# Attention row maxima from the high halves alone, two heads at a time in two 32-row groups of TensorE, with two score banks instead of three

## The chip, the cores and the metric

One core of one Trainium2 chip runs the whole kernel. The metric is the device time of one execution, in microseconds (us); lower is better.

## The reference, cut to what matters

The input x (2 x 1024 x 1024) is normalised over its last axis. Grouped-query attention follows: 32 query heads and 8 key/value heads of 32 numbers, rotary embedding, causal mask, softmax. A gated feed-forward net with 4-bit weights is computed from the same normalised x, and the two are joined:

```python
scores = einsum('bqhd,bkhd->bhqk', q, k) / sqrt(32) + causal_mask
attn = softmax(scores, axis=-1)
s = einsum('bhqk,bkhd->bqhd', attn, v) @ wo
x = x + s * silu(ffn(layernorm(x)))
```

The change touches only how the maximum of each row of scores is found, which the softmax subtracts before the exponential, and what stands around that.

## The kernel before

The stages run one after the other: project_qkv, attend, project_out, feed_forward. All products use numbers split into a 16-bit high half and a 16-bit low half. Only `attend` is changed, and `load_heads`, which fills its buffers.

**Tiling.** There are 64 heads in all (2 batches of 32). A step works on one head of 1024 positions, cut into ST = 8 tiles of 128, which are visited in ORDER = 7, 0, 6, 1, 5, 2, 4, 3. Four heads share one key head; `qT[:, u]` and `kT[:, u]` (u = 0 or 1) hold such a group of four. Their partitions are a stack of three pieces of 32 rows: q high with k high, q high with k low, q low with k high, so one matmul with 96 rows gives the full product.

**What a head costs.** `maxima` on TensorE computes, for query tile t, the scores of its 128 queries against keys 0 to (t+1)·128 into a PSUM tile (a wide one of 1024 columns and a narrow one of 512, in turn), adds the causal mask by a 128-column matmul (L670), and VectorE's `tensor_reduce` (L793) takes the negated maximum of each row: 8 such rounds in a head. When 8 are there, `turn_shifts` transposes the 8 columns (L654), ScalarE copies them out (L754), and SyncE sends them by DMA (L602) into row 96 of `qT`, against a row of ones in `kT`. So the score matmul with 97 rows (`scores`, L685) yields shifted scores, transposed (keys on partitions). There are 12 such chunks in a head, in 3 PSUM banks in turn, 8 of them with a mask matmul (L688). ScalarE takes the exponential of each chunk (L744) into `probs`. `probs` is split: its upper bits are the high half, and the low half `p_lo` is computed by GpSimd (POOL) in four parts of 1152, 1152, 1152 and 640 columns and by VectorE in one of 512 (all L580). `outputs` on TensorE (L712 to L716) multiplies both halves with the values, 80 matmuls of 32 to 65 columns in a head. ScalarE copies the result out (`copy_sums`, L764 and L766).

**Order.** Each engine runs its own program, in order. Step r of TensorE interleaves, over i = 0 to 7, `scores` of head r, `maxima` of head r+2, and `outputs` of head r-1; the transpose for head r+1 stands at i = 1. VectorE does the reductions of head r+2 and, after the first of them, its part of `p_lo` of head r-1. Waits are counting semaphores written by hand: maxima number n waits until number n-2 is reduced, a score chunk until the exponential three chunks back is done. The loop body holds 8 heads. The first 8 and the last 8 heads are written out, and the loop runs 6 times between them, so its body is jumped back to 5 times.

**Refill.** After the last score chunk of the fourth head of a group SyncE refills that half of `qT` and `kT` by 6 DMAs (`load_heads`, L91 and L92). The first `maxima` of the new group stand two to three steps later.

Of the kernel before, what the change touches and what calls it, by code (L numbers as in the profile page):

```python
# [7 lines left out]
ALU = mybir.AluOpType  # L8
# [506 lines left out]
def attend(nc, q_d, k_d, v_d, o_d, wo, ident, identb, maskb, qT, kT, qk_loaded, vn, v_loaded, o, o_stored, a, a_loaded,  # L515
# [7 lines left out]
    SC_BANKS = 3  # L523
# [5 lines left out]
    with ExitStack() as ctx:  # L529
# [3 lines left out]
        def sem(name):  # L533
# [6 lines left out]
        shift = sb("shift", [P, 2, ST], F16)  # L540
        shT = sb("shT", [P, 2, P], F16)
        sc_ps = [ctx.enter_context(nc.psum_tensor(f"sc_ps{i}", [P, BANK], F32)) for i in range(SC_BANKS)]
        mx_ps = [ctx.enter_context(nc.psum_tensor("mx_wide_ps", [P, FULL], F32)),
                 ctx.enter_context(nc.psum_tensor("mx_ps", [P, BANK], F32))]
# [6 lines left out]
        mx_taken = sem("mx_taken")  # L551
        shift_turned = sem("shift_turned")
# [16 lines left out]

        def chunks_to(t):  # L570

            return max(i + 1 for i, c in enumerate(SC) if c[0] == t)
# [10 lines left out]
        def steps(eng, step):  # L583

            for r in range(-3, 0):
                step(*at(0, 0, r, R))
# [9 lines left out]
        def _(sp):  # L596
            def send_shift(m, r):
                if not exists(m, r):
                    return
                h, u, q = head(m, r), r // REP, r % REP  # L600
                sp.wait_ge(shift_copied, h + 1)
                sp.dma_start(qT[STACK:STACK + 1, u, q, :], shT[STACK:STACK + ST, r % 2, :]  # L602
                             ).then_inc(shift_loaded[r % 2], 16)
# [26 lines left out]
            def step(m, r):  # L630
                send_shift(*at(m, r, 1, R))
# [14 lines left out]
        def _(pe):  # L646
            def turn_shifts(m, r):
                if not exists(m, r):
                    return
                h = head(m, r)  # L650
                pe.wait_ge(mx_taken, ST * (h + 1))
                if not isinstance(m, int) or h >= 1:
                    pe.wait_ge(shift_copied, h)
                pe.transpose(tr_ps[STACK:STACK + ST, 0:P], shift[:, r % 2, :], ident[:, :]).then_inc(shift_turned, 1)  # L654

            def maxima(m, r, i):
                if not exists(m, r):
                    return
                h, u, q, t = head(m, r), r // REP, r % REP, ORDER[i]
                if i == 0 and q == 0:  # L660
                    pe.wait_ge(qk_loaded[u], 96 * (m + 1))
                if not isinstance(m, int) or ST * h + i >= 2:
                    pe.wait_ge(mx_taken, ST * h + i - 1)
                n = (t + 1) * P
                bank = mx_ps[i % 2]
                for c in range(0, n, BANK):
                    e = min(c + BANK, n)
                    last = pe.matmul(bank[:, c:e], qT[0:STACK, u, q, t * P:(t + 1) * P], kT[0:STACK, u, c:e],  # L668
                                     start=True, stop=(e < n))
                last = pe.matmul(bank[:, t * P:n], identb[:, :], maskb[:, :], start=False, stop=True)  # L670
                last.then_inc(mx_ready, 1)

            def scores(m, r, i):
# [3 lines left out]
                if i == 0:  # L677
                    pe.wait_ge(shift_loaded[r % 2], 16 * ((R // 2) * m + r // 2 + 1))
# [55 lines left out]
        def _(act):  # L734
# [12 lines left out]
            def shifts(m, r):  # L747
                if not exists(m, r):
                    return
                h = head(m, r)  # L750
                act.wait_ge(shift_turned, h + 1)
                if not isinstance(m, int) or h >= 2:
                    act.wait_ge(shift_loaded[r % 2], 16 * ((R // 2) * m + r // 2))
# [1076 lines left out]
```

## Time and profile before

| what | value |
|---|---|
| median of 3 runs | 2586.61 us (2580.41 to 2593.28) |
| the profiled execution's own time | 2587.13 us |
| its span in the profile | 2584.2 us |
| PE (TensorE matmul) busy | 2391.5 us, 93% |
| DVE (VectorE) busy | 1550.2 us, 60% |
| POOL (GpSimd) busy | 942.3 us, 36% |
| ACT (ScalarE) busy | 748.2 us, 29% |

Times in profile rows count from the start of the span. The attention stage lies between about 389 and 932 us. A PE matmul record overlaps the next one, so that the pitch between two starts, and not the duration, tells what a matmul costs. The number in square brackets behind a row is the idle time of the engine just before it, with what ended it; "issue" means that the profile shows nothing that it waited for.

### The profile page before, as it was taken

The page shows a single profiled execution, that of the slowest core. Times are in us where ns is not written, and L with a number is a line of the kernel's source. Part 1 is how long each engine was busy: PE and PEld are TensorE (multiplying, and loading weights), DVE is VectorE, ACT ScalarE, POOL GpSimd, SP SyncE. Part 2 cuts the span into 40 slices and gives each one's busy share as a digit, 9 for nine tenths or more (in the row PEclk, how much of TensorE's full clock was granted, in tenths as well). Part 3 has the DMA queues.
Part 4 walks back from the last instruction along what each step waited for, and adds up shares of the span by engine and source line. Part 5 has one row for each costly group of instructions (what it writes and reads, how often), then busy time and mean ns, then how long its engine had stood idle before and what let it go on. Part 6 is the DMA issues. An engine that isn't in the chain of part 4 may idle for free.

```text
span 2584.2 us, 46178 instructions
## 1 busy us (share of the span) xinstructions
PE 2391.5 (93%) x17048; PEld 1234.9 (48%) x17048; DVE 1550.2 (60%) x2800; ACT 748.2 (29%) x1469; POOL 942.3 (36%) x619
## 2 busy tenths in 40 slices
PE   5877888999999959989999999999999999999997
PEld 3434435666666634434444444444444444444432
DVE  5533448888888848646555555555555555555566
ACT  3211115777777743212020202020202020202022
POOL 2433436999999940002020202020202020202035
PEclk8988998999999979999999999999999999999999
DMA  5222131222222145500000000000000000000046
GB/s 155 70 66 66 37 84 44 70 70 68 70 70 70 55 146 171 167 36 12 13 12 12 12 12 12 12 12 12 12 12 12 12 12 12 12 12 10 8 167 228
DMA packets 129662, 138.26 MB, mean 54 GB/s; under 512 B 33106, under 2 KB 106421, under 8 KB 129148
## 3 DMA queue, kind: packets, MB, share of 16 engines
q1 hardware_dynamic: 127228, 127.96, 16.3%
q10 hardware_dynamic: 2304, 8.39, 0.8%
q8 instruction: 103, 1.69, 0.3%
q14 instruction: 27, 0.22, 0.0%
HBM read 88.76 MB, written 47.42 MB: 53 GB/s over the span
## 4 chain that ended last, share of the span: by engine, by line
PE 51%; DVE 3%; issue 1%; ACT 0%; POOL 0%; DVEq 0%; POOLq 0%
PE dn_ps L1477 17%; PE gate_ps L1458 16%; PE up_ps L1458 16%; PE s_ps L1427 1%; DVE zero L1545 1%; DVE wf L1557 0%; DVE dif L1551 0%; PE s_ps L1435 0%; DVE acc L1589 0%; ACT arena L1639 0%; PE z_ps L1427 0%; DVE nib L1526 0%; DVE acc L1582 0%; DVE zhalf L1540 0%; DVE idf L1505 0%
## 5 line engine op out<-in xcount | busy, mean ns | idle before, releaser
L1458 PE MATMUL gate_ps<-xT,wg 128*128 128x512 f16 x2112 | 788.9, 381 | 3.8 <-POOL wg L1679 3.8
L1458 PE MATMUL up_ps<-xT,wg 128*128 128x512 f16 x2016 | 765.6, 380 | 0.0
L580 POOL TENSOR_TENSOR p_lo<-probs 128x1152 f16<-128x1152 f32 (+1 forms) x256 | 501.3, 1994 | 49.2 <-ACT probs L744 49.0
L1477 PE MATMUL dn_ps<-wd,hT 128*128 128x512 f16 (+1 forms) x2112 | 466.1, 380 | 3.1 <-DVE acc L1582 3.1
L1679 POOL TENSOR_TENSOR wg<-wf,wg 128x512 f16<-128x512 f32 (+1 forms) x88 | 99.7, 1134 | 870.4 <-ACT wg L1625 870.4
L744 ACT ACTIVATE probs<-sc_ps 128x512 f32<-128x512 f32 (+3 forms) x768 | 350.9, 490 | 124.3 <-PE sc_ps L688 105.9
L1477 PEld LDWEIGHTS dn_ps<-wd,hT 128*128 128x128 f16 (+1 forms) x2112 | 201.6, 98 | 265.4 <-issue 25.8
L1582 DVE TENSOR_TENSOR acc<-acc,dn_ps 128x512 f32<-128x512 f32 x320 | 219.6, 686 | 178.5 <-PE dn_ps L1477 178.3
L1458 PEld LDWEIGHTS gate_ps<-xT,wg 128*128 128x128 f16 x2112 | 208.6, 99 | 241.9 <-issue 9.8
L793 DVE TENSOR_REDUCE shift<-mx_wide_ps 128x1 f16<-128x1024 f32 (+3 forms) x256 | 261.9, 1023 | 85.0 <-PE mx_wide_ps L670 84.9
L1458 PEld LDWEIGHTS up_ps<-xT,wg 128*128 128x128 f16 x2016 | 197.6, 98 | 229.7 <-issue 2.2
L1565 DVE SCALAR_TENSOR_TENSOR arena<-up_ps,arena 128x512 f32<-128x512 f32 x84 | 58.1, 691 | 359.7 <-ACT arena L1639 359.7
L1625 ACT ACTIVATE wg<-wf 128x512 f16<-128x512 f32 (+1 forms) x88 | 54.6, 621 | 714.5 <-DVE wf L1557 714.5
L685 PE MATMUL sc_ps<-arena 97*128 97x512 f16 (+3 forms) x768 | 227.4, 330 | 14.8 <-issue 14.6
L491 PE MATMUL qk_ps<-xT,w 128*128 128x512 f16 x960 | 226.3, 399 | 0.0
L1693 POOL TENSOR_TENSOR hT<-arena,hT 128x512 f16<-128x512 f32 (+1 forms) x88 | 101.8, 1157 | 333.1 <-ACT hT L1642 333.1
L716 PE MATMUL o_ps<-arena,p_lo 128*128 128x33 f16 x2304 | 193.4, 179 | 0.0
L1545 DVE TENSOR_SCALAR zero<-zhalf 128x128 uint32<-128x128 uint32 (+2 forms) x544 | 175.4, 425 | 4.5
L1181 PE MATMUL out_ps<-wo,aT 128*128 128x512 f16 x768 | 171.0, 383 | 2.8 <-ACT wo L1007 2.8
L712 PE MATMUL o_ps<-arena,probs 128*128 128x65 f16 x1792 | 161.8, 192 | 3.8 <-POOL p_lo L580 3.8
L668 PE MATMUL mx_wide_ps<-arena 96*128 96x512 f16 (+3 forms) x512 | 139.3, 354 | 21.8 <-DVE arena L781 14.2
L716 PEld LDWEIGHTS o_ps<-arena,p_lo 128*128 128x128 f16 x2304 | 158.7, 96 | 0.7
(130 smaller groups left out, 2985.5 us busy)
## 6 DMA issues: line engine op xcount, KB each, us to landing
o_scratch<-o SPq DMA_DIRECT2D x16, 1040.0 KB, 4.9
a<-o_scratch SPq DMA_DIRECT2D x16, 1040.0 KB, 5.4
arena<-q_scratch SPq DMA_DIRECT2D x48, 256.0 KB, 3.4
arena<-in_qw_d SPq DMA_DIRECT2D x42, 256.0 KB
xin<-in_x SPq DMA_DIRECT2D x16, 512.0 KB, 6.1
s_scratch<-arena ACTq DMA_DIRECT2D x16, 512.0 KB, 2.6
xT<-in_x SPq DMA_DIRECT2D x32, 256.0 KB, 4.7
xT<-s_scratch SPq DMA_DIRECT2D x32, 256.0 KB, 5.7
```

The lines of the kernel that those rows point to most:

```text
L491: last = pe.matmul(qk_ps[e % QB][:, :], w[:, wp, s, j * P:(j + 1) * P], xT[:, xp, s, tc * BANK:(tc + 1) * BANK], start=(s == 0 and k == 0) ...
L580: eng.tensor_tensor(p_lo[:, r % 2, c], probs[:, r % 2, c], p_hi[:, r % 2, c], ALU.subtract).then_inc(done, 1)
L685: last = pe.matmul(bank[:, 0:e - c], kT[0:STACK + 1, u, t * P:(t + 1) * P], qT[0:STACK + 1, u, q, c:e], start=True, stop=(c > t * P))
L712: pe.matmul(o_ps[:, c:c + VW], hi, vn[:, u, k, :], start=first, stop=False)
L716: last = pe.matmul(o_ps[:, c:c + VH], lo, vn[:, u, k, 0:VH], start=False, stop=final)
L744: act.activation(probs[:, r % 2, START[t] + c:START[t] + e], sc_ps[n % SC_BANKS][:, 0:e - c], ACT.Exp, scale=float(1.0 / np.sqrt(HD))).the ...
L793: dve.tensor_reduce(shift[:, r % 2, t:t + 1], mx_ps[i % 2][:, 0:(t + 1) * P], AX_X, ALU.max, negate=True).then_inc(mx_taken, 1)
L1181: last = pe.matmul(out_ps[u][:, cols], aT[:, u, xp, s, :], w[:, wp, s, cols], start=(s == 0 and k == 0), stop=(s == KT - 1 and k == 2))
L1458: last = pe.matmul(to[q][:, :], wg[:, u, wp, s, g * P:(g + 1) * P], xT[:, xp, s, t * BANK:(t + 1) * BANK], start=(s == 0 and k == 0), stop ...
L1477: last = pe.matmul(dn_ps[n][:, :], hT[0:w, hp, e, tokens], wd[0:w, wp, e, n * BANK:(n + 1) * BANK], start=(e == 0 and p == 0), stop=(e == ...
L1545: last = dve.tensor_scalar(zero[0:p, :].rearrange("p (c k) -> p c k", k=HALF_NIB)[:, v, i], zhalf[0:p, v], 4 * i, 15, ALU.logical_shift_ri ...
L1582: dve.tensor_tensor(acc[:, k // 2, cols], acc[:, k // 2, cols], dn_ps[n][:, :], ALU.add).then_inc(dn_taken, 1)
```

## The change

Row maxima are computed from q high times k high alone (32 rows instead of 96), for two heads of a pair side by side. So that the two use different rows of TensorE's array, `load_heads` now stores the pieces of even and odd heads differently: rows 0 to 31 hold the high half of an even head and the low half of an odd one, rows 32 to 63 the reverse, both against k high; rows 64 to 95 hold q high against k low. The q pieces of the first two kinds need two DMAs each, so a refill has 8 DMAs instead of 6.

The maxima of a pair are cut into 12 units of at most 512 columns (`UNITS`). A unit is one matmul for each head of the pair, into the two banks of `mx_ps[k % 2]`, then, where the unit holds the diagonal, a mask matmul for each, and one `tensor_reduce` over both banks. Tiles over 512 columns have two units, whose results are joined by a small `tensor_tensor` with min over both heads at the end of the pair. The units of a pair whose first head is r stand at i = 6 and 7 of step r-4, at i = 0, 2, 3, 4, 6 and 7 of step r-3, and at i = 0, 2, 3 and 4 of step r-2; no unit stands at i = 1 and 5 of any step. Transpose, copy and DMA of the shifts are done once for a pair. The maxima now need 4 PSUM banks, and the scores have 2 banks instead of 3.

```diff
 def load_heads(...)
-    for piece, (qp, kp) in enumerate([(0, 0), (0, 1), (1, 0)]):
+    for piece, (qps, kp) in enumerate([((0, 1), 0), ((1, 0), 0), ((0,), 1)]):
         rows = slice(piece * HD, (piece + 1) * HD)
-        eng.dma_start(qT[rows, u, :, :], q_d[g, qp].rearrange("(r d) t -> d r t", d=HD)).then_inc(qk_loaded[u], 16)
+        turns = len(qps)
+        for e, qp in enumerate(qps):
+            eng.dma_start(qT[rows, u, :, :].rearrange("d (r e) t -> d e r t", e=turns)[:, e],
+                          q_d[g, qp].rearrange("(r e d) t -> e d r t", e=turns, d=HD)[e]).then_inc(qk_loaded[u], 16)
         eng.dma_start(kT[rows, u, :], k_d[g, kp]).then_inc(qk_loaded[u], 16)
...
-    SC_BANKS = 3
+    SC_BANKS = 2
+    LEAD = 6
+    UNITS = [(7, 0), (7, 1), (0, 0), (6, 0), (6, 1), (1, 0), (5, 0), (2, 0), (5, 1), (4, 0), (3, 0), (4, 1)]
+    NU = len(UNITS)
...
+        def unit_at(m, r, i):
+            slot = r % 2 * ST + i - LEAD
+            ahead = 4
+            if slot < 0:
+                slot, ahead = slot + 2 * ST, 2
+            if slot % 4 == 3:
+                return None
+            m, r = at(m, r - r % 2, ahead, R)
+            return (m, r, slot // 4 * 3 + slot % 4) if exists(m, r) else None
...
             def send_shift(m, r):
+                if r % 2 or not exists(m, r):
+                    return
-                sp.wait_ge(shift_copied, h + 1)
-                sp.dma_start(qT[STACK:STACK + 1, u, q, :], shT[STACK:STACK + ST, r % 2, :]
+                sp.wait_ge(shift_copied, pair(m, r) + 1)
+                sp.dma_start(qT[STACK:STACK + 1, u, q:q + 2, :], shT[STACK:STACK + 2 * ST, p, :]
...
+            def maxima(m, r, k):
+                u, q, n = r // REP, r % REP, NU * pair(m, r) + k
+                t, c = UNITS[k]
+                if k == 0 and q == 0:
+                    pe.wait_ge(qk_loaded[u], 128 * (m + 1))
+                if not isinstance(m, int) or n >= 2:
+                    pe.wait_ge(mx_taken, n - 1)
+                first, end = c * BANK, min((c + 1) * BANK, (t + 1) * P)
+                diagonal = end == (t + 1) * P
+                banks = mx_ps[k % 2]
+                for e in range(2):
+                    rows = slice(e * HD, (e + 1) * HD)
+                    last = pe.matmul(banks[:, e, 0:end - first], qT[rows, u, q + e, t * P:(t + 1) * P],
+                                     kT[rows, u, first:end], start=True, stop=not diagonal)
+                if diagonal:
+                    for e in range(2):
+                        last = pe.matmul(banks[:, e, t * P - first:end - first], identb[:, :], maskb[:, :],
+                                         start=False, stop=True)
                 last.then_inc(mx_ready, 1)
...
             def step(m, r):     
                 for i in range(ST):
                     scores(m, r, i)
-                    maxima(*at(m, r, 2, R), i)
+                    if unit_at(m, r, i):
+                        maxima(*unit_at(m, r, i))
+                    if r % 2 == 0 and i == LEAD + 1:
+                        turn_shifts(*at(m, r, 2, R))
                     if i == 1:
-                        turn_shifts(*at(m, r, 1, R))
...
-                    if i == 2:
+                    if r % 2 == 1 and i == 0:
                         shifts(*at(m, r, 1, R))
...
+            def maxima(m, r, k):
+                dve.wait_ge(mx_ready, NU * n + k + 1)
+                if k == 0 and (not isinstance(m, int) or n >= 2):
+                    dve.wait_ge(shift_turned, n - 1)
+                to = shift[:, p, :, t] if width + c * BANK == (t + 1) * P else part[:, p, :, t - BANK // P]
+                dve.tensor_reduce(to, mx_ps[k % 2][:, :, 0:width], AX_X, ALU.max, negate=True).then_inc(mx_taken, 1)
+                if k == NU - 1:
+                    dve.wait_ge(mx_taken, NU * (n + 1))
+                    dve.tensor_tensor(shift[:, p, :, BANK // P:ST], shift[:, p, :, BANK // P:ST], part[:, p, :, :],
+                                      ALU.min).then_inc(shift_done, 1)
```

## Rows read from the trace of the kernel before

**Rows 1.** Busy time by engine in 50 us of the attention stage:

```profile
450.00:500.00 50.00, 48.58 (x772) 33.60 (x773) 43.96 (x58) 39.62 (x95) 50.00 (x27) 1.00 0.24 70
```

**Rows 2.** Timeline of POOL over the stage (start, duration, idle before):

```profile
409.12 125.47 POOL L580 TENSOR_TENSOR p_lo<-probs 128x1152 f16<-128x1152 f32 x64 [28.19 <-ACT probs L744]
...
604.47 2.18 POOL L580 TENSOR_TENSOR p_lo<-probs 128x1152 f16<-128x1152 f32 x1 [3.60 <-ACT probs L744]
...
804.89 2.18 POOL L580 TENSOR_TENSOR p_lo<-probs 128x1152 f16<-128x1152 f32 x1 [2.85 <-ACT probs L744]
```

**Rows 3.** The page, costliest groups: the p_lo parts on POOL:

```profile
L580 POOL TENSOR_TENSOR p_lo<-probs 128x1152 f16<-128x1152 f32 (+1 forms) x256 | 501.3, 1994 | 49.2 <-ACT probs L744 49.0
```

**Rows 4.** Timeline of ACT, the last instruction of four successive heads' copy:

```profile
612.34 0.20 ACT L766 ACTIVATE o<-o_ps 128x33 f32<-128x33 f32 x1
...
619.62 0.20 ACT L766 ACTIVATE o<-o_ps 128x33 f32<-128x33 f32 x1
...
627.37 0.20 ACT L766 ACTIVATE o<-o_ps 128x33 f32<-128x33 f32 x1
...
635.22 0.20 ACT L766 ACTIVATE o<-o_ps 128x33 f32<-128x33 f32 x1
```

**Rows 5.** Timeline, one head: POOL's first and second part, VectorE's part:

```profile
644.87 2.55 POOL L580 TENSOR_TENSOR p_lo<-probs 128x1152 f16<-128x1152 f32 x1
...
647.39 2.10 POOL L580 TENSOR_TENSOR p_lo<-probs 128x1152 f16<-128x1152 f32 x1
...
644.10 1.36 DVE L580 TENSOR_TENSOR p_lo<-probs 128x512 f16<-128x512 f32 x1
```

**Rows 6.** Timeline of PE (starts give the pitch):

```profile
643.04 0.38 PE L685 MATMUL sc_ps<-arena 97*128 97x512 f16 x1
...
643.26 0.22 PE L668 MATMUL mx_ps<-arena 96*128 96x128 f16 x1
...
643.31 0.22 PE L670 MATMUL mx_ps<-maskb,identb 128*128 128x128 bf16 x1
...
643.46 0.22 PE L654 MATMUL tr_ps<-ident,shift 128*8 128x128 f16 x1
...
643.62 0.19 PE L714 MATMUL o_ps<-arena,probs 128*128 128x33 f16 x1
...
643.68 0.18 PE L716 MATMUL o_ps<-arena,p_lo 128*128 128x33 f16 x1
...
643.71 0.19 PE L712 MATMUL o_ps<-arena,probs 128*128 128x65 f16 x1
```

**Rows 7.** Timeline of PE at the loop's jump:

```profile
601.38 0.28 PE L685 MATMUL sc_ps<-arena 97*128 97x128 f16 x1 [3.11 <-issue]
```

**Rows 8.** TensorE's mean granted clock over the loop:

```profile
450.00:880.00 430.00, 405.51 (x6328) 280.10 (x6329) 358.31 (x471) 327.53 (x784) 409.12 (x210) 0.97 0.24 69
```

**Rows 9.** Timeline of ACT around the copy of sums:

```profile
642.64 0.55 ACT L764 ACTIVATE o<-o_ps 128x455 f32<-128x455 f32 x1
...
643.24 1.09 ACT L744 ACTIVATE probs<-sc_ps 128x512 f32<-128x512 f32 x2
```

**Rows 10.** Row maxima on VectorE, widest and narrowest shape:

```profile
L793 DVE TENSOR_REDUCE shift<-mx_wide_ps 128x1 f16<-128x1024 f32 x64 | 78.5, 1227 | 33.0 <-PE mx_wide_ps L670 33.0
...
L793 DVE TENSOR_REDUCE shift<-mx_ps 128x1 f16<-128x128 f32 x64 | 17.9, 280 | 0.0
```

**Rows 11.** Refill of q and k: first and last issue, landing of the three k:

```profile
634.22 0.34 SPq L91 DMA_DIRECT2D arena<-q_scratch  x1
...
636.68 0.38 SPq L92 DMA_DIRECT2D arena<-k_scratch  x1
...
DMA to landing us min/median/max: 2.6/3.3/5.1
```

**Rows 12.** Start of the stage: first maximum on VectorE, first score:

```profile
390.60 1.23 DVE L793 TENSOR_REDUCE shift<-mx_wide_ps 128x1 f16<-128x1024 f32 x1 [0.82 <-PE mx_wide_ps L670]
...
405.65 0.31 PE L685 MATMUL sc_ps<-arena 97*128 97x128 f16 x1
```

More of the change, by code:

```diff
@@ L539, in attend @@
         p_lo = sb("p_lo", [P, 2, COLS], F16)
-        shift = sb("shift", [P, 2, ST], F16)
+        shift = sb("shift", [P, 2, 2, ST], F16)
+        part = sb("part", [P, 2, 2, ST - BANK // P], F16)
         shT = sb("shT", [P, 2, P], F16)
         sc_ps = [ctx.enter_context(nc.psum_tensor(f"sc_ps{i}", [P, BANK], F32)) for i in range(SC_BANKS)]
-        mx_ps = [ctx.enter_context(nc.psum_tensor("mx_wide_ps", [P, FULL], F32)),
-                 ctx.enter_context(nc.psum_tensor("mx_ps", [P, BANK], F32))]
+        mx_ps = [ctx.enter_context(nc.psum_tensor(f"mx_ps{i}", [P, 2, BANK], F32)) for i in range(2)]
         o_ps = ctx.enter_context(nc.psum_tensor("o_ps", [P, BANK], F32))
@@ L583, in steps @@
         def steps(eng, step):
-            for r in range(-3, 0):
+            for r in range(-4, 0):
                 step(*at(0, 0, r, R))
@@ L649, in turn_shifts @@
                     return
[L650 to L670, printed above, removed]
+                n = pair(m, r)
@@ new lines, in turn_shifts @@
+                pe.wait_ge(shift_done, n + 1)
+                if not isinstance(m, int) or n >= 1:
+                    pe.wait_ge(shift_copied, n)
+                pe.transpose(tr_ps[STACK:STACK + 2 * ST, 0:P],
+                             shift[:, r // 2 % 2, :, :].rearrange("p h t -> p (h t)"), ident[:, :]
+                             ).then_inc(shift_turned, 1)
+            def maxima(m, r, k):
[16 more added lines that the diff above has]
+                                         start=False, stop=True)
@@ L749, in shifts @@
                     return
[L750 to L753, printed above, removed]
-                act.activation(shT[STACK:STACK + ST, r % 2, :], tr_ps[STACK:STACK + ST, 0:P], ACT.Copy
+                n, p = pair(m, r), r // 2 % 2
+                act.wait_ge(shift_turned, n + 1)
+                if not isinstance(m, int) or n >= 2:
+                    act.wait_ge(shift_loaded[p], 16 * ((R // 4) * m + r // 4))
+                act.activation(shT[STACK:STACK + 2 * ST, p, :], tr_ps[STACK:STACK + 2 * ST, 0:P], ACT.Copy
                                ).then_inc(shift_copied, 1)
@@ L784, in _ @@
             last.then_inc(zeros_set, 1)
-            def maxima(m, r, i):
-                if not exists(m, r):
-                    return
-                h, t = head(m, r), ORDER[i]
-                dve.wait_ge(mx_ready, ST * h + i + 1)
-                if i == 0 and (not isinstance(m, int) or h >= 2):
-                    dve.wait_ge(shift_turned, h - 1)
-                dve.tensor_reduce(shift[:, r % 2, t:t + 1], mx_ps[i % 2][:, 0:(t + 1) * P], AX_X, ALU.max,
-                                  negate=True).then_inc(mx_taken, 1)
+            def maxima(m, r, k):
+                n, p = pair(m, r), r // 2 % 2
+                t, c = UNITS[k]
+                width = min((c + 1) * BANK, (t + 1) * P) - c * BANK
+                dve.wait_ge(mx_ready, NU * n + k + 1)
[7 more added lines that the diff above has]
+                                      ALU.min).then_inc(shift_done, 1)
             def step(m, r):
                 for i in range(ST):
-                    maxima(*at(m, r, 2, R), i)
+                    if unit_at(m, r, i):
+                        maxima(*unit_at(m, r, i))
                     if i == 0:
```

15 lines of the change are left out of this document (9 added, 6 removed).

## The prediction

> **What bounds the kernel now.** The change touches one stage, so I read first how busy each engine is there. In a stretch of 50 us without a loop jump GpSimd (POOL) is busy for all of it, TensorE (PE) for 48.58, VectorE (DVE) for 43.96 and ScalarE for 39.62 [rows 1]. PE's share says little, since its records overlap; POOL's full 50.00 says that it never waits there. The timeline of POOL shows how far this goes: its first run of 64 parts of `p_lo` has no gap, and later it pauses only once a lap of the loop, by 3.60 us at 604.47 and 2.85 at 804.89 [rows 2]. In all it waited 49.0 us for ScalarE [rows 3], of which 28.19 lie before its first part; the other 20.8 belong to the five jumps, 4.2 each. Three laps of eight heads took 804.89 - 604.47 = 200.4 us, or 66.8 each [rows 2].
>
> The pace of a head, read from ScalarE's copies, has two values: 7.28 us soon after a jump (612.34 to 619.62), and then 7.75 and 7.85 (627.37 to 635.22) [rows 4]. The 7.85 is POOL's own pace: eight of them make 62.8, and POOL has no gap while it lasts. The 7.28 is PE's. PE is paced by the pitch between starts [rows 6]: 0.22 us for 512 columns, 0.05 for 128, 0.03 for the small output matmuls. A head's scores are 4608 columns, 1.96 us, and eight masks, 0.46. Its maxima are as much again. Its outputs are 80 matmuls at 0.027, 2.15, and its transpose is 0.31. The sum is 7.30.
>
> What ties PE to POOL's pace is VectorE's part of `p_lo`: it was issued at 644.10, took 1.36 us and ended 0.6 after POOL began its next part at 644.87, and that part took 2.55 us where its neighbour took 2.10 [rows 5]. So VectorE waits for the end of a part of POOL, and the reductions behind it come late. The Trainium skill (SBUF — State Buffer, "Who interferes with whom") has a VectorE instruction with two SBUF inputs and a GpSimd one that reads SBUF block each other for whole instructions; the trace agrees.
>
> At a jump PE stands still for about 3 us (3.11, for nothing that the profile shows) [rows 7], and the granted clock falls from 2.4 to 1.2 GHz: its mean of 0.97 over 430 us with five jumps [rows 8] is 26 us at half clock, 5.2 a jump, which cost about 2.6 us of work. PE's lap is so 8 x 7.30 + 3.0 + 2.6 = 64.0 us, POOL's 62.8, the measured one 66.8. PE and POOL are nearly level. Work taken from PE can give back at most the 20.8 us in which POOL waited, 0.8% of the kernel.
>
> **The change part by part.**
>
> *Products of the maxima.* For a pair there were 9216 columns, 3.92 us. Now each unit's two matmuls stand in different row groups, and if they overlap, 4608 columns count, 1.96, with one smallest pitch, 0.03, for each of the 12 seconds: 2.32. The trace shows no such matmul. Bounds: full overlap 1.96, none 3.92. I take overlap, since the two share neither rows, weights nor PSUM bank. The Trainium skill (TensorE: Matmul & The Clock Gate, "Measured speedup vs the span model") gives 3.07x for four row tiles at 512 columns. No run here shows it.
>
> *Masks.* 16 for a pair, as before: 0.93 us.
>
> *Switching the shape of the array.* A unit goes from full-height matmuls to 32-row ones and back, 24 times for a pair. The nearest row is the transpose, with 8 weight columns: it starts 0.15 us after a 128-column mask matmul, and the next starts 0.16 after it, where 128 columns otherwise have 0.05 to 0.06 [rows 6]. So each change of shape costs 0.095. 24 of them are 2.28 us a pair. Bounds: nothing (if row groups switch freely) and 0.19 (if weights too must then be loaded in the open). I take 0.095. The Trainium skill (TensorEngine Tiling (Array Packing), "Key Properties") says that changing the tiling mode drains TensorE: it speaks against this change, and the transpose's two pitches agree.
>
> *Transpose.* One for a pair in place of two: 0.31. The maxima with transpose then are 2.32 + 0.93 + 2.28 + 0.31 = 5.84 a pair, 2.92 a head, against 2.42 + 0.31 = 2.73. PE gains nothing: 7.30 becomes 7.5, or 7.3 if the seconds start at once. I take 7.40.
>
> *Two score banks.* A chunk now waits for the exponential two chunks back. The tight place is tile 6's chunk, which waits for the first half of tile 0. ScalarE, busy with the copy from 642.64, takes the two halves from 643.24, 0.55 us each [rows 9], so the first is done 0.8 us after PE began the second half at 643.04 [rows 6]. Until now 1.13 us of work stood between; with no unit at i = 1 and the transpose gone it is 0.22 + 20 x 0.027 = 0.76, and PE is earlier by 0.1 at tile 0. That is a wait of 0.15; three other places miss by 0 to 0.05. I take 0.2 a head, between 0 and 0.6 (one whole exponential). PE's pace becomes 7.6, still under 7.85.
>
> *VectorE.* A reduction costs 0.145 us and 1.057 ns a column, from 1227 ns at 1024 and 280 at 128 [rows 10]. A head's eight cost 6.03; twelve units for a pair 11.48, or 5.74 a head. The 0.3 saved lies behind PE and POOL: nothing. The new min has two SBUF inputs too, so once a pair it waits for POOL, up to a part of 2.1 us, which VectorE's spare time covers (7.85 - 5.74 - 0.7), and holds POOL up by little: a tenth of what the 512-column part does (0.45) is 0.04, 32 times 1.3 us. Bounds 0 and 14.
>
> *The refill.* It starts after the fourth head's last score chunk and was not urgent before. Now the first unit of the new group stands at i = 6 of the very next step, some 6.3 us later at PE's pace (7.30 less the 1.0 of one slot), 6.9 at POOL's. The six DMAs were issued from 634.22 to 636.68, and the last k landed 5.1 later [rows 11]: 7.6 us in all, already too late. Two more issues at 0.49 make it 8.6 at most; the bytes are the same, so 8.2. PE stands 1.7 us, once a lap, in the middle; everything behind it in PE's order (scores, outputs) waits too. The other refill of a lap hides behind the jump.
>
> *Start.* Before the first score VectorE must reduce the first pair's units and six of the next: 11.5 + 5.8 = 17.3 us from 390.60 [rows 12], so 408.0 against 405.65. That is 2.2 us later, and POOL's first part with it.
>
> **The sum.** PE's lap: 8 x 7.6 = 60.8, jump 3.0, slow clock 2.2 (fewer columns to slow), refill 1.7: 67.7 us. It is over POOL's 62.8, so it is the lap: 0.9 more than 66.8, five times 4.5 us. In the two stretches of eight before the first jump POOL keeps 7.85 and loses what the refill exceeds its 0.6 of lead, about 1.1 each: 2.2. Start 2.2, min 1.3. Together 10.2 us on the profiled execution's own 2587.13 (span 2584.2 and 2.9 around it; the median of the runs is 0.5 lower): 2597 us.
>
> **The rivals.** *Cheaper switches.* If changing the row groups costs nothing, PE's pace is 7.6 - 1.1 = 6.5, with more waiting for ScalarE 6.7. Its lap is 53.6 + 3.0 + 2.2 + 2.3 = 61.1, under POOL's 62.8; POOL then loses about 1.2 a lap, five laps gain 2.8 each, 14 us, less 3.5 for start and min: 2577; with nothing lost at jumps and start, 2566. For it: 32-row matmuls keep all columns, unlike the transpose. Against it: the transpose's switch cost the same going in and coming out. It decides from about 0.03 a switch.
>
> *No overlap.* If the two matmuls of a unit run one behind the other, PE needs 0.8 to 1.0 us a head more, 8.5 against POOL's 7.85. Each lap grows by another 7.5 us, and the 24 heads outside by 0.65: 2597 + 37 + 15 = 2649. With half the overlap PE's pace is 8.05 and it is 2620. It decides where PE passes 7.85.
>
> *Nothing moves.* PE's waits for ScalarE and for the refill could be smaller than taken, and POOL's 7.85 hides the rest: 2583 to 2590.
>
> **How the numbers follow.** The forecast (2590 to 2606) has 0.45, cheaper switches 0.22, little or no overlap 0.15, nothing moves 0.18. A measurement here can tell about 0.5%, 13 us, from no change. Faster than 2574 is most of the first rival: 0.20. Slower than 2600 is the second rival and somewhat under half of the forecast's own spread, 0.38. The rest, 0.42, is within 0.5%. The range, from 2571 (inside the first rival) to 2630 (past half overlap), leaves out some 2 in 10.
>
> **What the profile would show.** Right: starts of the two matmuls of a unit about 0.03 us apart, and some 0.1 us extra before and after each unit; a head's pace of about 7.6 after a jump; a PE gap of 1 to 2 us before the first unit at i = 6 of a lap's fifth step; POOL gaps of about 5 us a lap; the first score near 408. Wrong: a pitch of 0.2 between the two matmuls of a unit; no extra around it; or POOL without a gap at the jumps.

## The result and the profile after

The changed kernel takes 2627.39 us, the median of 4 runs (2624.13 to 2629.98), against 2588.28 (2580.41 to 2593.28) for the kernel before on the same chip: 1.0153 times as long, 95% interval 1.0125 to 1.0182. Forecast were 2597 us and a range of 2571 to 2630. The direction and the mechanism came out, the size did not: 39 us are lost, not 10. Ratios are taken from fast executions alone; of all executions below only two of x2_same_rows count as slow (2781.74 us, the profiled one, and 2821.41), which stand in its median and not in its ratio.

The profiled execution has a span of 2628.2 us, 44.0 more than before. POOL's first part of `p_lo` starts 1.8 us later (410.89 against 409.12), the time from that part to the last one grows from 522.3 us to 559.4, by 37.1, and what follows the stage takes 1658.0 us against 1652.8. The last is no effect of the change: that same code took between 1650 and 1660 us in the profiles of this study. The loss lies in the attention stage.

Busy time by engine in the 50 us of [rows 1]; the columns are the stretch, then PE, weight loads, VectorE, ScalarE and POOL with their instructions, the granted clock as a share of 2.4 GHz, the DMA share and GB/s:

```profile
450.00:500.00 50.00, 47.73 (x738) 28.07 (x737) 43.14 (x47) 37.23 (x89) 45.62 (x25) 1.00 0.16 49
```

POOL was busy for all 50.00 and now is for 45.62, at the same full clock. PE also has fewer instructions done (738, not 772). So even without a jump and without a slow clock PE now sets the pace. POOL's timeline, to set against [rows 2] (the bracket is the idle time before the row):

```profile
410.89 4.31 POOL L602 TENSOR_TENSOR p_lo<-probs 128x1152 f16<-128x1152 f32 x2 [30.50 <-ACT probs L774]
...
549.50 2.11 POOL L602 TENSOR_TENSOR p_lo<-probs 128x1152 f16<-128x1152 f32 x1 [3.76 <-ACT probs L774]
...
601.77 7.45 POOL L602 TENSOR_TENSOR p_lo<-probs 128x1152 f16<-128x1152 f32 x4 [0.42 <-ACT probs L774]
610.18 7.45 POOL L602 TENSOR_TENSOR p_lo<-probs 128x1152 f16<-128x1152 f32 x4 [0.96 <-ACT probs L774]
621.87 2.11 POOL L602 TENSOR_TENSOR p_lo<-probs 128x1152 f16<-128x1152 f32 x1 [4.24 <-ACT probs L774]
```

Where a run of 64 parts had no gap, POOL now pauses within the lap as well, often after every head (four parts, 7.45 us). From 549.50 to 621.87 a lap lasts 72.37 us. The page's group of these parts, which answers to [rows 3]:

```profile
L602 POOL TENSOR_TENSOR p_lo<-probs 128x1152 f16<-128x1152 f32 (+1 forms) x256 | 484.6, 1920 | 105.3 <-ACT probs L774 103.8
```

POOL waited 103.8 - 30.5 = 73.3 us for ScalarE after its first part, against 20.8. Of these 52.5 us more, 16.7 are no loss: the parts got that much shorter (484.6 busy, not 501.3; four parts take 7.45 us, not 7.85). The 0.4 is about what the part of 2.55 in [rows 5] has over its neighbour. That POOL, now waiting for probabilities, meets VectorE's part less often is the likely reason; no run sets it apart. The other 35.8 are nearly all of the stage's 37.1.

ScalarE's last copy of four successive heads, as in [rows 4]:

```profile
566.88 0.20 ACT L796 ACTIVATE o<-o_ps 128x33 f32<-128x33 f32 x1
...
574.85 0.21 ACT L796 ACTIVATE o<-o_ps 128x33 f32<-128x33 f32 x1
...
582.81 0.21 ACT L796 ACTIVATE o<-o_ps 128x33 f32<-128x33 f32 x1
...
592.22 0.20 ACT L796 ACTIVATE o<-o_ps 128x33 f32<-128x33 f32 x1
```

A head takes 7.97 and 7.96 us, and the one with the refill 9.41. Four places in PE's timeline: the first score (beside [rows 12]), the jump (beside [rows 7]), the stop for the refill, and last a unit between its neighbours (beside [rows 6]):

```profile
407.77 0.31 PE L713 MATMUL sc_ps<-arena 97*128 97x128 f16 x1
...
546.72 0.28 PE L713 MATMUL sc_ps<-arena 97*128 97x128 f16 x1 [2.92 <-issue]
...
588.92 0.39 PE L693 MATMUL mx_ps<-arena 32*128 32x512 f16 x2 [1.07 <-DMA arena<-k_scratch]
...
600.35 0.38 PE L713 MATMUL sc_ps<-arena 97*128 97x512 f16 x1
...
600.86 0.19 PE L742 MATMUL o_ps<-arena,probs 128*128 128x33 f16 x1
...
601.51 0.22 PE L716 MATMUL sc_ps<-identb,maskb 128*128 128x128 bf16 x1
...
601.66 0.39 PE L693 MATMUL mx_ps<-arena 32*128 32x512 f16 x2
...
601.99 0.20 PE L740 MATMUL o_ps<-arena,probs 128*128 128x65 f16 x1
```

Two matmuls of a unit are merged into one row (x2) of 0.39 us, where a single one has 0.38 to 0.39: the second starts 3 ns after the first, by the starts in the trace. The unit begins 0.15 us after the mask matmul, where the usual pitch is 0.055, and what follows begins 0.33 after the unit, where 512 columns have 0.22. So a change of shape costs about 0.09 going in and 0.10 coming out. The Trainium skill (TensorE: Matmul & The Clock Gate, "Measured speedup vs the span model") has each further tile of a pack add about 4 ns to its span; the 3 ns of this trace agree. The Trainium skill (TensorEngine Tiling (Array Packing), "Key Properties") has a change of tiling mode drain the engine; the 0.09 and 0.10 us before and after a unit agree.

The rows at 600.35 and 600.86 show a wait that stands in no group of PE on the page: the first outputs of the step, which stand right behind the scores of i = 1, start 0.51 us after a 512-column chunk, not 0.22. ScalarE's timeline has what they wait for, the copy of the previous outputs, which ends at 600.72:

```profile
600.08 0.56 ACT L794 ACTIVATE o<-o_ps 128x455 f32<-128x455 f32 x1
600.53 0.19 ACT L796 ACTIVATE o<-o_ps 128x33 f32<-128x33 f32 x1
```

Two laps after, and one before, in the columns of [rows 1], show the clock:

```profile
549.50:621.87 72.37, 66.94 (x966) 39.12 (x964) 55.70 (x60) 49.45 (x116) 60.39 (x32) 0.90 0.20 62
621.87:692.85 70.98, 65.86 (x966) 38.53 (x964) 56.26 (x60) 49.46 (x116) 60.55 (x32) 0.93 0.21 64
```

```profile
604.47:671.51 67.04, 62.74 (x973) 43.43 (x971) 54.53 (x73) 50.22 (x120) 62.42 (x32) 0.96 0.23 67
```

A mean of 0.90 over 72.37 us is 14.5 us at 1.2 GHz, 0.93 over 70.98 is 9.9, and 0.96 over 67.04 was 5.4. The first of these laps has a second slow stretch, of 3.4 us, right behind the refill's stop at 588.92:

```profile
586.00:598.00 12.00, 10.93 (x154) 6.52 (x152) 8.85 (x10) 7.80 (x19) 9.98 (x6) 0.86 0.13 36
```

After a jump two heads are now slow (11.5 and 11.3 us on average over the five); before, they took 11.0 and, the second, 8.7 to 9.9.

The stage also starts at 1.2 GHz, and stays there longer. POOL's first two heads, in the changed kernel and then in the kernel before:

```profile
410.89:430.83 19.94, 19.85 (x183) 9.37 (x183) 12.81 (x15) 12.15 (x28) 15.05 (x8) 0.61 0.01 2
```

```profile
409.12:424.80 15.68, 14.90 (x193) 9.51 (x192) 13.22 (x17) 12.21 (x30) 15.54 (x9) 0.97 0.01 3
```

They take 4.3 us more, at a mean clock of 0.61 and not 0.97.

### The profile page after: what moved, and what is told of

Same layout as the page of the kernel before. It is cut to its first block, busy times and chain, and to the rows that moved or that the text cites. A ratio compares the mean times of both kernels' runs of the same rounds, so it can differ in the third digit from the quotient of the medians.

```text
span 2628.2 us, 45726 instructions
## 1 busy us (share of the span) xinstructions
PE 2433.3 (93%) x17016; PEld 1201.6 (46%) x17016; DVE 1557.3 (59%) x2704; ACT 743.9 (28%) x1437; POOL 925.2 (35%) x619
## 4 chain that ended last, share of the span: by engine, by line
PE 51%; DVE 3%; issue 1%; ACT 0%; POOL 0%; DVEq 0%; POOLq 0%
PE dn_ps L1512 18%; PE gate_ps L1493 16%; PE up_ps L1493 15%; PE s_ps L1462 1%; DVE zero L1580 1%; DVE wf L1592 0%; DVE dif L1586 0%; PE s_ps L1470 0%; ACT arena L1674 0%; PE z_ps L1462 0%; DVE acc L1624 0%; DVE nib L1561 0%; DVE zhalf L1575 0%; DVE idf L1540 0%; PE z_ps L1470 0%
## 5 line engine op out<-in xcount | busy, mean ns | idle before, releaser
L602 POOL TENSOR_TENSOR p_lo<-probs 128x1152 f16<-128x1152 f32 (+1 forms) x256 | 484.6, 1920 | 105.3 <-ACT probs L774 103.8
L1512 PE MATMUL dn_ps<-wd,hT 128*128 128x512 f16 (+1 forms) x2112 | 471.7, 383 | 3.1 <-DVE acc L1617 3.1
L713 PE MATMUL sc_ps<-arena 97*128 97x512 f16 (+3 forms) x768 | 245.5, 347 | 22.6 <-issue 16.3
L824 DVE TENSOR_REDUCE shift<-mx_ps 128x2 f16<-128x1024 f32 (+3 forms) x256 | 204.3, 827 | 31.9 <-PE mx_ps L697 27.7
L824 DVE TENSOR_REDUCE part<-mx_ps 128x2 f16<-128x1024 f32 x128 | 156.7, 1224 | 76.4 <-PE mx_ps L693 76.0
L740 PE MATMUL o_ps<-arena,probs 128*128 128x65 f16 x1792 | 168.6, 195 | 2.1 <-POOL p_lo L602 2.1
L744 PEld LDWEIGHTS o_ps<-arena,p_lo 128*128 128x128 f16 x2304 | 164.6, 98 | 9.2 <-issue 1.6
```

The source lines that it names most:

```text
L602: eng.tensor_tensor(p_lo[:, r % 2, c], probs[:, r % 2, c], p_hi[:, r % 2, c], ALU.subtract).then_inc(done, 1)
L713: last = pe.matmul(bank[:, 0:e - c], kT[0:STACK + 1, u, t * P:(t + 1) * P], qT[0:STACK + 1, u, q, c:e], start=True, stop=(c > t * P))
L740: pe.matmul(o_ps[:, c:c + VW], hi, vn[:, u, k, :], start=first, stop=False)
L744: last = pe.matmul(o_ps[:, c:c + VH], lo, vn[:, u, k, 0:VH], start=False, stop=final)
L824: dve.tensor_reduce(to, mx_ps[k % 2][:, :, 0:width], AX_X, ALU.max, negate=True).then_inc(mx_taken, 1)
L1512: last = pe.matmul(dn_ps[n][:, :], hT[0:w, hp, e, tokens], wd[0:w, wp, e, n * BANK:(n + 1) * BANK], start=(e == 0 and p == 0), stop=(e == ...
```

## The experiments

Each kernel is compared with the kernel before on the same chip. In the expectations A is my account at that point; the letters behind it are its rivals for that run. "Stage" is the time from POOL's first part of `p_lo` to its last in the profile: 522.3 us before, 559.4 after.

| label | device us, median (range) | ratio to before, 95% interval | stage, us |
|---|---|---|---|
| after | 2627.39 (2624.13 to 2629.98) | 1.0153 (1.0125 to 1.0182) | 559.4 |
| x1_full_rows | 2612.74 (2611.35 to 2621.45) | 1.0101 (1.0078 to 1.0124) | 537.6 |
| x2_same_rows | 2756.32 (2731.56 to 2821.41) | 1.0568 (1.0541 to 1.0594) | 706.1 |
| x3_later_lead | 2603.35 (2601.42 to 2604.2) | 1.0054 (1.0038 to 1.0071) | 539.5 |
| x7_full_rows_later | 2592.85 (2590.7 to 2597.37) | 1.0026 (1.0015 to 1.0037) | 528.8 |
| x4_before_two_banks | 2596.10 (2589.55 to 2600.89) | 1.0026 (1.0015 to 1.0037) | 527.1 |
| x6_no_join | 2625.47 (2621.34 to 2634.94) | 1.0150 (1.0124 to 1.0177) | 561.0 |
| x5_before_high_only | 2991.40 (2984.71 to 2992.05) | 1.1549 (1.1526 to 1.1572) | 920.9 |
| x9_before_64_rows | 2988.28 (2983.63 to 2991.09) | 1.1553 (1.1533 to 1.1572) | 923.2 |
| x8_before_no_mask | 2593.38 (2591.34 to 2598.12) | 1.0022 (1.0011 to 1.0033) | 530.3 |
| y1_before_unrolled | 2565.34 (2563.08 to 2567.86) | 0.9920 (0.9904 to 0.9937) | 503.1 |
| y2_after_unrolled | 2591.82 (2588.31 to 2602.24) | 1.0031 (1.0016 to 1.0047) | 525.0 |
| y3_later_lead_unrolled | 2573.85 (2569.69 to 2575.47) | 0.9947 (0.9931 to 0.9964) | 510.4 |

**x1_full_rows**: the changed kernel with the full product of 96 rows in each maximum, so no change of shape, but twice the columns.

```diff
-                    rows = slice(e * HD, (e + 1) * HD)
+                    rows = slice(0, STACK)
```

> The changed kernel, but both matmuls of a unit use all 96 rows (the full three-term product, as before the change), so no shape of the array is switched and nothing overlaps. Account A (switches and overlap nearly cancel, and the loss comes from PE's waits for ScalarE, the refill and the longer slow clock): a pair gains 24 switches at 0.097 us and loses 1.96 us of overlap, so a head is about 0.15 us cheaper and PE has more columns in a cold stretch; 2600 to 2620 us, against 2627. Account B (the overlap carries the maxima, the switches are cheap): a head becomes up to 0.96 us dearer; 2680 us or more.

It is 14.6 us faster than the changed kernel. PE's timeline, one unit of 256 columns:

```profile
597.78 0.22 PE L716 MATMUL sc_ps<-identb,maskb 128*128 128x128 bf16 x1
597.83 0.38 PE L693 MATMUL mx_ps<-arena 96*128 96x256 f16 x2
```

The unit begins 0.05 us after the mask matmul, not 0.15. So the extra belongs to the change of shape. Its stage is 21.8 us shorter; its profile reached the stage some 5 us later than the others do, in code that is the same, and its first units took about 3 us longer. Twice the columns (1.96 us more a pair) cost less than 24 changes at 0.095 (2.28 us) and a longer slow clock together (mean clock over 430 to 870 us 0.98, and 0.93 in the changed kernel).

**x2_same_rows**: both heads of a unit in the same 32 rows, so that they can't overlap. Its second head's maxima are of other numbers.

```diff
-                    rows = slice(e * HD, (e + 1) * HD)
+                    rows = slice(0, HD)
```

> The changed kernel, but both matmuls of a unit use rows 0 to 31, so they can't overlap while the switches stay. For odd heads the maxima are then made from the low half, so the shifts differ a little. Account A (PE bound at 7.96 us a head, the two matmuls start 3 ns apart in the profile): the second matmul shows its own pitch, 0.22 us at 512 columns, a head costs 0.96 us more, 64 heads 61 us: 2685 to 2695 us. Account B (PE is not the bound, waits hide it): under 2650 us.

It is far slower than A says, and its executions spread over 90 us. One unit of it on PE at full clock, and two stretches in the columns of [rows 1]:

```profile
707.27 0.60 PE L693 MATMUL mx_ps<-arena 32*128 32x512 f16 x2
```

```profile
560.00:600.00 40.00, 37.59 (x328) 17.66 (x327) 17.31 (x21) 16.66 (x39) 20.63 (x11) 0.50 0.17 53
700.00:740.00 40.00, 39.42 (x535) 21.31 (x534) 28.95 (x35) 27.39 (x64) 32.98 (x19) 0.98 0.18 56
```

The pair takes 0.60 = 0.38 + 0.22: one behind the other. At full clock a head takes 8.75 to 8.85 us, which is 7.96 and the 0.8 to 1.0 that the prediction gave to no overlap. But long stretches run at 1.2 GHz, with 13.5 to 14.3 us a head. They begin at the loop's jumps; before the first one (450 to 500 us) the clock is 1.00. These rows are of the execution of 2781.74 us, but the shortest one, of 2731.56, has a mean clock of 0.930 over its whole span too, where the kernel before has 0.963 to 0.967. That the two matmuls of a pair overlap is shown; what the overlap is worth is more than its columns.

**x3_later_lead**: every unit two slots later, the transpose with them, and ScalarE's copy of the shifts two places later. Units then stand at i = 0, 1, 2, 4, 5 and 6 of each step.

```diff
-    LEAD = 6
+    LEAD = 8
-                    if r % 2 == 0 and i == LEAD + 1:
-                        turn_shifts(*at(m, r, 2, R))
+                    if r % 2 == 1 and i == 1:
+                        turn_shifts(*at(m, r, 1, R))
-                    if r % 2 == 1 and i == 0:
+                    if r % 2 == 1 and i == 2:
```

> The changed kernel, but the units of a pair start two slots later (first unit at i = 0 of step r-3, last at i = 6 of step r-2), and the transpose stands at i = 1 of step r-1, as before the change, with ScalarE's copy at i = 2. Account A: the wait of 1.1 us for the refilled keys in every fourth step goes (8 times, 9 us, with the slow clock that follows it), and the transpose fills part of the wait for ScalarE; 2598 to 2614 us. Account B (the refill is hidden in PE's pace anyway): within 5 us of 2627.

As A says: 24.0 us of the 39 are back. PE has no wait for a refill any more, and POOL runs through most of a lap (28 parts in 54.8 us, 7.83 a head):

```profile
554.66 54.82 POOL L602 TENSOR_TENSOR p_lo<-probs 128x1152 f16<-128x1152 f32 x28 [0.43 <-ACT probs L774]
612.39 2.25 POOL L602 TENSOR_TENSOR p_lo<-probs 128x1152 f16<-128x1152 f32 x1 [2.92 <-ACT probs L774]
```

So the largest part of the loss comes from where the units stand, not from what they cost. The edit moves two things at once, the time that a refill has and the work between PE's waits for ScalarE; the waits of y2 and y3 below tell how they divide.

**x7_full_rows_later**: the edits of x1 and x3 together.

> Both edits together: units with all 96 rows (no shape switches, no overlap) and the units two slots later with the transpose at i = 1. If the losses add up as account A has them (refill and filler 24 us, switches with the slow clock 15 us), little is left of the 39 us: 2585 to 2594 us, level with the kernel before. If the two edits take back the same loss (say both only shorten the slow clock), it stays near the better of them: 2600 us.

2592.85 us: 34.5 of the 39 us are back, against 14.6 + 24.0 for the two alone, so they add up but for 4 (but for 6 by the ratios, which compare on the same chip). What is left, 0.26%, is what the next kernel has too.

**x4_before_two_banks**: the kernel before with two banks for the scores.

```diff
-    SC_BANKS = 3
+    SC_BANKS = 2
```

> The kernel before with two score banks instead of three and nothing else. Account A: at i = 1 a maximum, its mask and the transpose, 0.37 us, still stand between the scores and the outputs, so PE waits for ScalarE by little, and POOL's pace of 7.85 us hides it, but for the heads after a jump; 2588 to 2596 us. Account B (the missing third bank alone makes the 0.4 us of waits a head): 2610 us or more.

The third bank is worth 0.26% there, about 7 us, at the upper end of A. That POOL's 7.85 us a head hides the rest is A's account, which the time fits.

**x6_no_join**: the changed kernel without the min; PE's transpose waits for the last reduction instead. It leaves out the maximum over all keys but the last unit's in the tiles of two units.

```diff
                 if k == NU - 1:
-                    dve.wait_ge(mx_taken, NU * (n + 1))
-                    dve.tensor_tensor(shift[:, p, :, BANK // P:ST], shift[:, p, :, BANK // P:ST], part[:, p, :, :],
-                                      ALU.min).then_inc(shift_done, 1)
```

> The changed kernel without the small min that joins the two units of a wide tile: it leaves out the maximum over the keys before the last 512 (the shift is then the maximum of the unit with the diagonal). Account A (PE bound; VectorE has time to spare for its wait on POOL): 2620 to 2628 us. Account B (the min, which waits for POOL's part to end and holds POOL up, costs a part of the loss): below 2617 us.

No difference that can be told (2625.47). In the changed kernel the min took 1.06 us for 8 columns on each partition, which lies in VectorE's spare time:

```profile
604.90 1.06 DVE L827 TENSOR_TENSOR shift<-shift,part 128x8 f16<-128x8 f16 x1
```

Most of that seems to be waiting for POOL's part: in x1, before POOL's first part, the same min took 0.16:

```profile
408.47 0.16 DVE L827 TENSOR_TENSOR shift<-shift,part 128x8 f16<-128x8 f16 x1
```

**x5_before_high_only** and **x9_before_64_rows**: the kernel before with maxima of 32 rows, and of 64, instead of 96, everything else as it was. x5 leaves out the two products with a low half, x9 one of them.

```diff
-                    last = pe.matmul(bank[:, c:e], qT[0:STACK, u, q, t * P:(t + 1) * P], kT[0:STACK, u, c:e],
+                    last = pe.matmul(bank[:, c:e], qT[0:HD, u, q, t * P:(t + 1) * P], kT[0:HD, u, c:e],
```

```diff
-                    last = pe.matmul(bank[:, c:e], qT[0:STACK, u, q, t * P:(t + 1) * P], kT[0:STACK, u, c:e],
+                    last = pe.matmul(bank[:, c:e], qT[0:2 * HD, u, q, t * P:(t + 1) * P], kT[0:2 * HD, u, c:e],
```

> The kernel before with its maxima from rows 0 to 31 alone (high times high), one head at a time as before: switches without overlap, three score banks, no change to the refill. Account A: 16 switches a head at 0.095 us take PE from 7.28 to 8.8 us a head, which is over POOL's 7.85: at least 60 us slower, 2650 us or more, and more still if PE stays at its low clock as it did where both matmuls used the same rows. Account B (switches are cheap against what surrounds them): below 2620 us.

> The kernel before with its maxima from rows 0 to 63 (q high times k high and k low). The version with rows 0 to 31 ran the whole stage at 1.2 GHz and took 14.49 us a head. If the switching of the shape holds the clock down, this one stays there as well: 2980 to 3000 us. If it is the few rows at work, the clock comes back and the head costs 8.8 us: 2650 to 2720 us.

Both lose 15.5%. From 430 to 870 us, x5 first, then x9:

```profile
430.00:870.00 440.00, 436.06 (x3635) 193.66 (x3634) 198.16 (x271) 195.71 (x452) 227.59 (x120) 0.50 0.12 36
```

```profile
430.00:870.00 440.00, 435.89 (x3631) 194.17 (x3630) 197.71 (x270) 195.15 (x451) 227.77 (x121) 0.50 0.12 36
```

TensorE is granted 1.2 GHz for the whole stretch, although PE is busy for 436 of its 440 us, and a head takes 14.5 us. The kernel before holds 0.97 there, and differs only in the rows of its maxima. The stage starts at 1.2 GHz in every kernel here; these two never leave it. That 32 and 64 rows give the same to 0.1% speaks against an effect that grows with the rows left unused. Changes of shape alone don't explain it either, for the changed kernel has 12 a head (these two have 16) and is at 1.00 from 450 to 500 us. What holds the clock down stays open.

**x8_before_no_mask**: the kernel before without the mask matmuls in the maxima, so that the maximum is taken over masked keys too.

```diff
-                                     start=True, stop=(e < n))
-                last = pe.matmul(bank[:, t * P:n], identb[:, :], maskb[:, :], start=False, stop=True)
+                                     start=True, stop=True)
```

> The kernel before without the mask matmuls of its maxima: it leaves out the causal mask there, so the shift is the maximum over up to 127 keys more, an upper bound. It takes 0.46 us a head from PE and nothing from POOL. Account A (POOL bound at 7.85 us, PE's gain only shortens POOL's waits at the five jumps, 20.8 us in all): 2572 to 2585 us. Account B (PE was the bound): 64 times 0.46 us, 2561 us or less. Account C (VectorE's lock on POOL eats it all): 2586 to 2592 us.

A miss of A, which has PE's time as the bound behind a jump, and of the other two as well (C, the nearest, ended at 2592): PE has some 0.4 us of work less a head, and the kernel is 0.22% slower. A lap of it has these figures, where before had 0.96:

```profile
604.00:671.00 67.00, 60.24 (x902) 39.65 (x903) 55.17 (x70) 49.46 (x120) 61.58 (x32) 0.93 0.23 68
```

The second head behind a jump takes 11.0 to 11.3 us, where before had 8.7 to 9.9. With less to do PE gets the slow clock for longer, and that takes back more than it saved there: the third head behind the jump is faster (6.9 us, before 7.3), the second slower by 1.9.

**y1_before_unrolled**, **y2_after_unrolled**, **y3_later_lead_unrolled**: the loop over laps written out, in the kernel before, in the changed one, and in x3.

```diff
-            with eng.Fori(1, NH // R - 1) as m:
+            for m in range(1, NH // R - 1):
```

> The kernel before with the loop of attention written out, so that it never jumps back. The account of the prediction: POOL then keeps 7.85 us a head from the first to the last, and its 20.8 us of waits at the five jumps go: 2562 to 2572 us. Rival: the stop is the fetch of instructions, which a longer program has too, or POOL loses the time elsewhere: 2580 us or more.

> The changed kernel, the loop written out. If what the change costs sits mostly in the stretches at slow clock behind the jumps (about 3.4 us of each lap's 4.9), it comes to within 15 us of the kernel before with its loop written out. If it sits in the pace of a head and the refill, some 25 us stay between them; the time is 2588 to 2596 us.

> The changed kernel with the units two slots later, the transpose at i = 1, and the loop written out. Away from the jumps the version with the loop ran at 7.55 to 8.05 us a head, 7.7 in the mean, against 7.85 of the kernel before. If that pace holds, it beats both: 2555 to 2568 us. If the clock falls at the refills instead, 2575 us or more.

y1 is faster than both kernels, by 0.8% of before (0.63 to 0.96%). All but the first of POOL's 256 parts are one run without a gap:

```profile
410.95 500.68 POOL L580 TENSOR_TENSOR p_lo<-probs 128x1152 f16<-128x1152 f32 x255 [0.34 <-ACT probs L744]
```

The 20.8 us that POOL waited at the five jumps are gone, and that is the whole gain: 0.8% of 2588 is 20.7. The mean clock over 430 to 870 us is 1.00 in all three. y2 keeps 26.5 us to y1 where the loops have 39.1: roughly a third of the loss lay behind the jumps, two thirds in the pace. Its waits on PE from 430 to 870 us, some 54 heads (total us, times, longest), and then those of y3:

```profile
PEld o_ps L742 <- ACT o L796: 15.9, 41, 0.4
PEld sc_ps L713 <- ACT probs L774: 9.0, 30, 0.3
...
PEld mx_ps L693 <- DMA arena<-k_scratch: 5.9, 11, 1.2
```

```profile
PEld sc_ps L713 <- ACT probs L774: 18.4, 83, 0.3
```

The view names only the larger waits. A shorter one shows in PE's starts alone, as here in y2, where a score chunk starts 0.12 us after an output instead of 0.025, and 0.05 after the end of the exponential that frees its bank:

```profile
606.50 0.18 PE L744 MATMUL o_ps<-arena,p_lo 128*128 128x33 f16 x1
606.62 0.39 PE L713 MATMUL sc_ps<-arena 97*128 97x512 f16 x1
```

Added up from the starts (what a score chunk, or the first output of a step, is late by over its usual pitch, from 450 to 870 us), y2 waits 21.1 us for exponentials and 12.0 for the copy of the outputs, 0.41 and 0.23 us a head, beside the refill's 0.11 by the view. In 153 us of the changed kernel's laps at full clock the same count gives 0.23 and 0.24 a head. In y3 the copy and the refill are gone, and exponentials hold PE up for 19.4 us, 0.36 a head.

y3's time lies between the two accounts, 6 us over A's range and 1 under B's, and B's reason did not come: the clock is at 1.00. Its heads take 7.68 and 8.03 us in turn, a mean of 7.85, which is POOL's pace, so that PE is no longer the bound. It is 0.5% faster than the kernel before, and yet 8.5 us above y1. 7.2 of these lie in the stage, and in its first four heads: POOL starts at 409.47 and has done them at 448.03, in 38.56 us where four heads at its pace take 31.4; after that it has no gap. So the loss goes with the slow clock at the start of the stage, which lasts until 434 us here and until 410 in y1:

```profile
409.47:433.80 24.33, 24.17 (x203) 11.39 (x202) 14.65 (x17) 12.99 (x30) 17.26 (x9) 0.50 0.01 2
```

## Why the prediction was right, and where it fell short

The mechanism of the likeliest case decided: PE, not POOL, sets the pace of the changed kernel, because switches of shape eat what the overlap saves while two banks and the early refill add waits. Its time did not: it had 2590 to 2606 us, and 2627.39 is 21 above. That the time lies within the stated range, 2.6 us under its end, is in part luck, for the range was drawn up to 2630 for half the overlap, and the overlap was whole. The other cases fell: cheap switches (a switch cost 0.09 to 0.10), no overlap (the pair starts 3 ns apart), nothing moves. The signs named for being right came but for two sizes: POOL's gaps are 12.0 us in the lap from 549.50 (60.39 busy of 72.37), not 5, and a head's pace is 7.96, not 7.6. Point by point:

- **Products of the maxima.** Right and a little dear: 3 ns for each second matmul, not 0.03 us, so 2.0 us a pair instead of 2.32. x2 shows the overlap by taking it away.
- **Switching.** 0.095 was taken, 0.094 and 0.10 measured; x1 shows that it is the shape, for with 96 rows the extra is gone.
- **Waits for ScalarE with two banks.** This term was mis-sized. I took 0.2 us a head, with 0.6 as the upper bound; by PE's starts it is 0.47 in the laps (0.23 for exponentials, 0.24 for the copy) and 0.64 in y2 (0.41 and 0.23). The exponentials I had about right for the laps. I had put the other wait at nothing: with no unit and no transpose at i = 1 the first outputs come so soon after the scores that they wait for ScalarE's copy of the sums (600.86 in the rows above). With the measured terms the pace would be 7.30 + 0.06 for maxima and switches + 0.47 = 7.8; it is 7.96, so 0.1 to 0.2 a head has no name yet. Against the 7.6 foretold that is 2.9 us a lap. And since 7.96 is over POOL's 7.85, each of the 24 heads outside the laps pays too, where I had POOL hide it.
- **Slow clock.** The second mis-sized term. I took 2.2 us a lap, less than before because there were fewer columns to slow. The two heads behind a jump lose 3.8 besides the stop, and a lap has some 12 us at half clock, not 5: 10.2 behind the jump, and 3.4 behind the refill in every second lap. (By my own rule, half the time at 1.2 GHz, 12 us would have cost 6; what the clock costs is not simply that.) x8 shows how wrong the reasoning was: less work for PE made the slow stretch longer, not cheaper. The slow clock at the start of the stage I had at nothing; it costs 4.3 us in the first two heads.
- **Refill.** Right in place and nearly in size: PE stands 1.07 us before the first unit of a new group (8 times over the stage, 6.9 us in all in the list of waits), and with its echo in the next head a lap loses 1.2 us on average (1.8 and 0.6 in turn), against 1.7 taken.
- **Jump.** 2.92 us (3.11 before), as taken.
- **VectorE and the min.** Right: 1.06 us a pair, hidden, and x6 gains nothing that its runs can tell. The 1.3 us put down for it are too few to show there.
- **Start.** The first score at 407.77, foretold 408.0; POOL's first part 1.8 us later, 2.2 taken. Some of this is luck: VectorE's first reduction came at 389.55, 1.05 us earlier than before, and from there to the first score it is 18.2 us, not 17.3.

The lap in these terms: 8 x 7.96 = 63.7, jump 3.0, slow clock 3.8, refill 1.2, together 71.7, as measured (mean of 72.37 and 70.98), against 67.7 foretold and 66.8 before. Slow clock and refill are read from the lengths of these same heads, so the sum has to close; what it adds is how the loss divides. Five laps lose 24.5 us instead of 4.5, the start 1.8, and the heads outside the laps 37.1 - 24.5 = 12.6 instead of 2.2. 4.3 of the 12.6 are the first two heads at the slow clock; the rest is the pace over 7.85 and the refills. The pace is not the same everywhere: heads of the written-out parts, first and last, take 8.07 to 8.16 us when nothing stops them, those of the loop's body 7.96, before its first jump too. y2, written out throughout, has 8.07 to 8.15, so it goes with the written-out form and not with the place. Its waits for exponentials are longer by as much (0.41 a head, not 0.23); why is open.

Seen by experiments rather than by terms, the 39 us are: placement of the units, 24 (x3), which takes away the refill's wait, 8 us or so, and the wait for the copy of the outputs, 0.24 us a head and so by my estimate some 15 over 64 heads, but not the waits for exponentials; shape changes net of the columns that they save, and the clock that goes with them, 15 (x1); and the lost bank, 7 at most (x4), for x7 with its two banks ends on the same ratio as x4. That the lost bank accounts for what x7 leaves is argued from the equal numbers; a changed kernel with three banks was not tried. How the 24 divide between refill and copy was read from waits and not run apart.

## What to carry to other kernels

Before work is saved on an engine, ask what its switch to the cheaper form costs and at which clock: here half the columns bought 24 changes of shape a pair and slower stretches, and the full product with unchanged shape was faster. When work is taken out of a place in an in-order program, list every wait behind that place, copies of results as well as operand buffers: the work removed was what had hidden them. And where the trace shows idle time only at a loop's jumps, write the loop out first: it gained 21 us, when a change of all the arithmetic lost 39.

## What the runs showed of the hardware that was not expected

Maxima of 32 or of 64 rows, one at a time between full-height matmuls, hold TensorE at 1.2 GHz, at which the stage begins, for the whole of it (0.50 over 440 us in x5 and x9, 14.5 us a head for 7.85), with PE busy for 99% of it. Pairs of 32 rows that overlap keep 2.4 GHz away from jumps and refills (1.00 from 450 to 500 us), pairs that do not overlap fall to 1.2 GHz at jumps and stay there for long stretches (x2), and 96 rows keep 2.4 GHz but for short stretches (x1, 0.98 from 430 to 870 us).

Rows of 32 also lengthen the slow stretch at the start of the stage. x3, and then x7, which differs from it only in its full 96 rows:

```profile
414.00:430.00 16.00, 16.00 (x141) 7.75 (x139) 9.03 (x12) 8.57 (x20) 11.18 (x7) 0.50 0.01 2
```

```profile
414.00:430.00 16.00, 15.40 (x205) 9.66 (x206) 13.76 (x16) 12.73 (x30) 15.72 (x9) 1.00 0.01 3
```

After a jump the length of the slow stretch does not follow PE's work: 3.4 or 6.8 us before, 10.2 in the changed kernel (17.1 after the last jump), and longer than before when 0.4 us of mask matmuls a head are left out (clock 0.93, not 0.96, over 67 us). What sets it was not found.
